# Second output banks, an earlier norm and transfers moved ahead in the first feed-forward group of a sandwich block

## What is computed

```python
x = x + layernorm(attn(layernorm(x), Wq, Wk, Wv, Wo))
x = x + layernorm(ffn(layernorm(x), gate_cp, up_cp, down_cp))
```

## Time and profile before

| | before |
|---|---|
| median of 3 runs | 719.9 us (717.62 to 720.74) |
| the profiled execution | 722.85 us |
| its span | 721.0 us |
| TensorE busy | 667.9 us, 93% of the span |
| VectorE busy | 491.9 us, 68% |
| GpSimd busy | 440.1 us, 61% |
| ScalarE busy | 373.6 us, 52% |
| DMA, mean | 159 GB/s |
| granted TensorE clock, mean | 0.972 of full |

### The profile page before, as it was taken

The page is one execution under the profiler, slowest core; times in us unless marked ns, Lnnn a source line. Parts: engine busy times, 40 slices in busy tenths (PEclk is TensorE's granted clock), DMA queues, the critical chain, the costliest instruction groups (busy, mean ns, idle before and its releaser), DMA issues. The chain is left out here.

```text
span 721.0 us, 16306 instructions
## 1 busy us (share of the span) xinstructions
PE 667.9 (93%) x5872; PEld 468.7 (65%) x5872; DVE 491.9 (68%) x977; ACT 373.6 (52%) x651; POOL 440.1 (61%) x615
## 2 busy tenths in 40 slices
PE   5898899999999999999977689999999999999896
PEld 3686686878778786877863346565665656665464
DVE  7657964479635885366577677877878788865542
ACT  3532332333323332333347567778777787777642
POOL 6098958628585576970245456667666666666542
PEclk9898999999999999999998799999999999999999
DMA  6835447415482246830299564657475757646222
GB/s 216 327 99 177 152 162 257 151 30 174 167 263 85 90 146 190 282 103 16 66 248 282 124 171 119 175 163 191 149 193 160 190 147 188 155 132 183 79 78 98
DMA packets 65549, 114.98 MB, mean 159 GB/s; under 512 B 12624, under 2 KB 29136, under 8 KB 65488
## 3 DMA queue, kind: packets, MB, share of 16 engines
q1 hardware_dynamic: 65488, 114.16, 53.8%
HBM read 81.76 MB, written 32.37 MB: 158 GB/s over the span
## 5 line engine op out<-in xcount | busy, mean ns | idle before, releaser
L1420 POOL TENSOR_TENSOR act<-inter,act 128x512 f16<-128x512 f32 x128 | 157.9, 1240 | 93.4 <-ACT act L1460 93.3
L1464 ACT ACTIVATE gated<-gbank,c_gate 128x512 f32<-128x512 f32 x128 | 87.4, 683 | 56.9 <-PE gbank L1622 56.9
L1537 DVE SCALAR_TENSOR_TENSOR inter<-ubank,c_up,gated 128x512 f32<-128x512 f32 x128 | 95.8, 748 | 28.4 <-ACT gated L1464 24.2
L1664 PE MATMUL ybank<-down,act 128*128 128x160 f16 x512 | 109.8, 234 | 0.0
L1666 PE MATMUL ybank<-down,act 128*128 128x160 f16 x512 | 109.1, 233 | 0.0
L1665 PE MATMUL ybank<-down,act 128*128 128x160 f16 x512 | 109.1, 233 | 0.0
L1460 ACT CAST act<-inter 128x512 f16<-128x512 f32 x128 | 78.0, 609 | 4.2 <-DVE inter L1537 4.2
L1664 PEld LDWEIGHTS ybank<-down,act 128*128 128x128 f16 x512 | 50.0, 98 | 29.5 <-issue 25.7
L1622 PE MATMUL ubank<-z,s_all 128*32 128x512 f16 x512 | 52.4, 399 | 17.9 <-DVE inter L1537 16.6
L1622 PE MATMUL gbank<-z,s_all 128*32 128x512 f16 x512 | 52.9, 403 | 5.6 <-DMA z<-token_features 3.8
L687 DVE SCALAR_TENSOR_TENSOR tu_lo<-chain,tu_hi 128x512 fp32r<-128x512 f32 x32 | 22.1, 691 | 45.0 <-ACT tu_hi L555 44.9
(11 more groups left out here) (196 smaller groups left out, 1911.4 us busy)
## 6 DMA issues: line engine op xcount, KB each, us to landing
x_ln<-x SPq DMA_DIRECT2D x64, 256.0 KB, 3.5
z<-token_features SPq DMA_DIRECT2D x64, 256.0 KB, 5.1
job<-job_in SPq DMA_DIRECT2D x24, 640.0 KB, 4.1
shared<-x SPq DMA_DIRECT2D x32, 256.0 KB, 2.8
x<-shared SPq DMA_DIRECT2D x32, 256.0 KB, 2.0
token_features<-z_hi SPq DMA_DIRECT2D x32, 256.0 KB, 3.8
x_res<-x SPq DMA_DIRECT2D x32, 256.0 KB, 2.9
out<-x_res SPq DMA_DIRECT2D x32, 256.0 KB, 3.0
```

Source lines behind the costliest of these rows:

```text
L1420: pool.tensor_tensor(hidden[par][:, i, TOK:2 * TOK], inter[:, i % INTERS, :], hidden[par][:, i, 0:TOK], ALU.subtract).then_inc(inter_ready, 1)
L1464: act.activation(gated[:, slot % 2, :], gbank[:], ACT.Silu, scale=c_gate[:]).then_inc(silu_done, 1)
L1537: dve.scalar_tensor_tensor(out=inter[:, i % INTERS, :], in0=ubank[:], scalar=c_up[:], in1=gated[:, i % 2, :], op0=ALU.mult, op1=ALU.mult). ...
L1664: pe.matmul(out, hidden[par][:, r, high], box[:, 0], start=False, stop=False)
```

## The change

Five edits, all in the lists' order or in the banks:

- In group 0 the odd steps 3 to 15 put gate and up in ybank0 and ybank1 (`pair_of`). From step 4 to 15 gate waits for the silu of step n-2 and up for the product of step n-2. Step 3 waits in their place for attention's last read of those banks (`y_read`). The silu of steps 3 to 15 waits also for the product of n-2, since its own output has two buffers. Steps 16 and 17 wait in full again.
- In group 0 the norm of tile m+1 moves from the end of step s == 3 to s == 2, behind the copy of the turned tile m, and its high and low halves move from s == 0 of the next round to s == 3, ahead of tile m's `z_high` and `z_low`.
- `load_z` of group 0's first half moves from t == 4 to t == 2 of attention's stores.
- x_ln of tile 8 goes ahead of the twelve reads of the down weights (now `jobs`); and in round 2 of every group `load_z` of the second half goes behind that round's output store and reload.
- ScalarE waits for `wov_done` 1 instead of 2 ahead of the exponentials.

```diff
--- before.py
+++ after.py
@@ -351,7 +351,7 @@
                         feats.load(sp, x1_t, XR + t, t)
                     if not more and t == 0:
                         feats.spill(sp, 1, 0)
-                    if not more and t == 4:
+                    if not more and t == 2:
                         sp.wait_ge(chain_done, b * CHAIN + 3 * K)
                         ffn_in.load_z(sp, feats, 0, 0, 0)
                 if more:
@@ -594,7 +594,7 @@
                         turned_hi(b, m)
                     if isinstance(b, int) and b == 0 and m == 2:
                         wov_hi(1)
-                act.wait_ge(wov_done, 2)
+                act.wait_ge(wov_done, 1)
                 if not more:
                     feats.high(act, 0)
                 for m in range(K):
@@ -1311,6 +1311,10 @@
         o_normed = sem("o_normed")
         out_ready = sem("out_ready")
 
+        def pair_of(n):
+            return ybank if isinstance(n, int) and n in range(3, I, 2) else (gbank, ubank)
         def schedule(engine, quad, loop=True):
 
 
@@ -1356,25 +1360,32 @@
                 else:
                     load_res(g + 1, q - 2)
 
-            def regroup(g, par, half, loads_before):
-                spread(g, par, half, loads_before)
-                ffn_in.load_z(sp, feats, g, par, half)
             def spread(g, par, half, loads_before):
 
                 sp.wait_ge(z_loaded[1 - par][half], loads_before * 64)
                 feats.spill(sp, half, g, 1 - par)
+            def jobs():
+                attention.jobs_stored(sp)
+                for b in range(I // PER):
+                    sp.dma_start(w_box[:, b * PER:(b + 1) * PER], d_dram[b][:, 0:PER]).then_inc(ffn_in.down_loaded, 16)
+                    for c in range(2):
+                        bank, quarter = (2 * b + c) // 4, (2 * b + c) % 4
+                        sp.dma_start(w_mom[:, bank, :, quarter * P:(quarter + 1) * P], d_dram[b][:, PER + c, :, 0:P]
+                                     ).then_inc(ffn_in.down_loaded, 16)
+                attention.all_stored(sp)
 
             def quad(g, par, count, j, made, begun, more):
                 for ahead in ((0,), (1, 2, 3), (), ())[j] if more else ():
                     m = g * Q + ahead + AHEAD + 2
                     sp.wait_ge(feats.h_normed, m - RING + 1)
                     feats.load(sp, x1_t, m, (ahead + AHEAD + 2) % RING)
+                if isinstance(g, int) and g == 0 and j == 0:
+                    jobs()
                 last = isinstance(g, int) and g == GROUPS - 1
                 if j == 2 and not last:
-                    regroup(g + 1, 1 - par, 1, count)
+                    spread(g + 1, 1 - par, 1, count)
                 for i in range(4 * j, 4 * j + 4):
                     for before, q in outputs(g, i, 2):
                         finish(before, q)
@@ -1384,7 +1395,8 @@
                 if j == 1 and not last:
                     if isinstance(g, int) and g == 0:
                         spread(g + 1, 1 - par, 0, count)
-                    ffn_in.load_z(sp, feats, g + 1, 1 - par, 0)
+                if j in (1, 2) and not last:
+                    ffn_in.load_z(sp, feats, g + 1, 1 - par, j - 1)
 
             sp.wait_ge(feats.h_normed, Q)
             feats.load(sp, x1_t, Q + 3, 3)
@@ -1394,14 +1406,6 @@
             attention.store(sp)
             for q in range(2):
                 load_res(0, q)
-            attention.jobs_stored(sp)
-            for b in range(I // PER):
-                sp.dma_start(w_box[:, b * PER:(b + 1) * PER], d_dram[b][:, 0:PER]).then_inc(ffn_in.down_loaded, 16)
-                for c in range(2):
-                    bank, quarter = (2 * b + c) // 4, (2 * b + c) % 4
-                    sp.dma_start(w_mom[:, bank, :, quarter * P:(quarter + 1) * P], d_dram[b][:, PER + c, :, 0:P]
-                                 ).then_inc(ffn_in.down_loaded, 16)
-            attention.all_stored(sp)
             schedule(sp, quad)
             finish(GROUPS - 2, Q - 1)
             reload(GROUPS - 2, Q - 1)
@@ -1461,7 +1465,9 @@
 
             def silu_at(n, slot):
                 act.wait_ge(gate_done, n + 1)
-                act.activation(gated[:, slot % 2, :], gbank[:], ACT.Silu, scale=c_gate[:]).then_inc(silu_done, 1)
+                if isinstance(n, int) and 3 <= n < I:
+                    act.wait_ge(inter_done, n - 1)
+                act.activation(gated[:, slot % 2, :], pair_of(n)[0][:], ACT.Silu, scale=c_gate[:]).then_inc(silu_done, 1)
 
             def moment_hi(g, bank):
 
@@ -1504,8 +1510,11 @@
                         moment_hi(g - 1, 1)
                     if i == I - 1:
                         moment_hi(g, 0)
-                    if s == 0 and made:
+                    first = isinstance(g, int) and g == 0
+                    if s == 0 and made and not (first and j):
                         feats.high(act, g * Q + j + AHEAD)
+                    if s == 3 and first and j < Q - 1:
+                        feats.high(act, j + AHEAD + 1)
                     if isinstance(n, int) and n == 2 * Q + 3:
                         attention.jobs_stored(act)
                     if s == 3 and made:
@@ -1534,7 +1543,7 @@
                 dve.wait_ge(up_done, n + 1)
                 if not (isinstance(n, int) and n < INTERS):
                     dve.wait_ge(inter_ready, n - INTERS + 1)
-                dve.scalar_tensor_tensor(out=inter[:, i % INTERS, :], in0=ubank[:], scalar=c_up[:],
+                dve.scalar_tensor_tensor(out=inter[:, i % INTERS, :], in0=pair_of(n)[1][:], scalar=c_up[:],
                                          in1=gated[:, i % 2, :], op0=ALU.mult, op1=ALU.mult).then_inc(inter_done, 1)
 
             def moment_lo(g, bank):
@@ -1579,13 +1588,18 @@
                         o_stats(before, q)
                     for before, q in outputs(g, i, 2):
                         o_finish(before, q)
-                    if s == 0 and made:
+                    first = isinstance(g, int) and g == 0
+                    if s == 0 and made and not (first and j):
                         feats.low(dve, m)
+                    if s == 2 and first:
+                        feats.norm(dve, m + 1, (j + 1 + AHEAD) % RING)
+                    if s == 3 and first and j < Q - 1:
+                        feats.low(dve, m + 1)
                     if s == 0 and begun:
                         feats.stats(dve, m + 1, (j + AHEAD + 1) % RING, loads)
                     if s == 3 and made:
                         feats.z_low(dve, m, (j + 2) % Q, z_banks, par if j < 2 else 1 - par)
-                    if s == 3 and begun:
+                    if s == 3 and begun and not first:
                         feats.norm(dve, m + 1, (j + 1 + AHEAD) % RING)
 
             product(0, 0)
@@ -1614,8 +1628,13 @@
                 if i % HALF == 0:
                     pe.wait_ge(z_loaded[par][i // HALF], count * 64)
                 side, c = i // HALF, i % HALF
-                for w, bank, free, done in ((GATE, gbank, silu_done, gate_done), (UP, ubank, inter_done, up_done)):
-                    if not (isinstance(n, int) and n == 0):
+                gate, up = pair_of(n)
+                if isinstance(n, int) and n == 3:
+                    attention.y_read(pe)
+                for w, bank, free, done in ((GATE, gate, silu_done, gate_done), (UP, up, inter_done, up_done)):
+                    if isinstance(n, int) and 3 < n < I:
+                        pe.wait_ge(free, n - 1)
+                    elif not (isinstance(n, int) and n in (0, 3)):
                         pe.wait_ge(free, n)
                     for u in range(4):
                         rows = slice(32 * u, 32 * u + 32)
```

## The result

| | before | after |
|---|---|---|
| median | 720.32 us (717.62 to 724.32, 4 runs) | 713.43 us (712.47 to 713.94, 4 runs) |
| ratio | 1 | 0.9897, 95% interval 0.9873 to 0.9922 |
| profiled execution, its span | 722.85, 721.0 us | 713.47, 711.6 us |
| VectorE's last instruction starts at | 717.78 | 708.37 |

The change makes the kernel 6.9 us faster by the medians. Between the two profiled executions it is 9.4 us, because that of before lies 2.5 us above its median. Three marks on VectorE's timeline split the 9.41 us by which the last instruction moved. The first statistics of y in attention's last body moved from 354.13 to 350.24, 3.89 us. From there to the first moments of group 0 (`mom_lo`, the low part of its first moment products, which VectorE forms near the group's end) it takes 64.00 instead of 67.61 us, 3.61 less.

The account below looks back on a forecast made before the run. Later groups were taken as bound by TensorE's own work, leaving gains in group 0, its change-over and attention's first body. 1.2 + 6.5 = 7.7 us took the median from 719.9 to 712.2 us, range 709.5 to 716.8.

Parts of the forecast that it names:

- Body 0: Attention's first body: the first exponential starts up to 3.2 us earlier, GpSimd's list limits the gain to 1.2 us.
- rival 3: Attention's first body gives nothing, eaten by GpSimd's list and a clock drop: 713.4 us, or 1.6 more; chance 0.17.
- Change-over: From attention to group 0: z read 3.9 us earlier, TensorE's wait for it gone, silu and product 1.1 us earlier.
- the prediction's lower bound for this term: Change-over from attention to group 0: gain of nothing, if the residual reads that z's reads pass come late.
- Round 0: Group 0's first round: the product of step 6 comes 2.2 us earlier, 1.1 more than the start gave.
- Round 1 and 2: Group 0's rounds: norm and halves lie beside copy and feature products, so a round takes 6.35 us instead of 8.73.
- x_ln of tile 8: Group 0, round 1: with its read ahead of the down weights, VectorE's stall of 2.98 us is gone or nearly.
- Crowding: Group 1's input: x_ln reads of tiles 9 to 11 still under way add 0.7 us to its load.
- A new wait for z: Group 1's first gate, round 3: TensorE's wait of 0.60 us becomes some 5 us and caps the gain.
- Later groups: Groups after group 0: nothing is shorter, and the second half's load moving by about a microsecond costs nothing.
- The page against the banks: A skill page reporting no further gain from PSUM double-buffering; by its rule group 0's rounds stay at 8.73 us.
- the first rival: Banks and new order do nothing for group 0's rounds, another wait takes the loop's place: 714.0 us; chance 0.15.

Follow-up runs that it names:

- e8_z_t3: Changed kernel with group 0's load of z one step later on SyncE's list, behind the first residual read and ahead of the second: 713.37 us, 0.9894 of before.
- e2_z_t4: Changed kernel with group 0's load of z back behind the two residual reads, at step 4 instead of 2: 714.34 us, 0.9919 of before.
- e5_x8_behind: Changed kernel with the read of x_ln for tile 8 again behind the twelve reads of the down weights: 718.58 us, 0.9961 of before.
- e10_no_round_edits: Changed kernel with both round edits undone (single banks, old place of norm and halves): 715.30 us, 0.9931 of before.
- e6_regroup: Changed kernel with the second half's load of group input again directly behind its spread, ahead of that quarter's output stores: 716.80 us, 0.9945 of before.
- e3_one_bank: Changed kernel with single banks for gate and up in group 0 again, new order of norm and halves kept: 714.10 us, 0.9915 of before.
- e7_wov_only: Kernel before with only the wait ahead of the first exponential changed, to one part of Wv instead of both: 719.63 us, 0.9986 of before.

## Why the prediction was right

The time, 713.43 against 712.2, came out because terms that were too large and terms that were too small made up for each other. Step by step:

- *Body 0, 1.2 us.* Right in size by the first statistics of y (1.5 on average) and by the medians (1.0 and 1.7). What it lacked is the clock: I had it as a loss in rival 3, "or 1.6 more". In the profiles with the edit it mostly stayed at 2.4 GHz through the products of y, and A gained 1.4 more, by luck as far as is shown; the profile of after has the earliest A of all. That GpSimd's list was the bound fits the 1.5 of a possible 3.2, and no run tests it.
- *Change-over, 1.1 us.* Wrong. The step that failed is "The other reads and stores behind z are 1.9 us later in SyncE's list; VectorE uses the first of them more than 5 us after". The issue did come 1.94 us later against the first statistics of y (15.25 instead of 13.31). What I left out is the landing: behind the four reads of z, this read took 6.8 us instead of 3.5, so it landed 5.2 us later in all, and VectorE waited 2.35 us for it. In e8_z_t3, where it goes ahead of z, it took 4.1 us and nobody waited. e2_z_t4 shows the sum as nothing; the prediction's lower bound for this term had named the reason.
- *Round 0, another 1.1 us.* Wrong in sign. Product 6 moved by 3.06 us where the last body's first statistics had moved by 3.89, so change-over and round 0 together lost 0.8. "VectorE is packed up to product 3" took the lengths from a trace in which GpSimd came second. And product 4 came 1.67 us behind product 3 instead of the 0.9 that I gave it, 0.95 of it a wait for its silu.
- *Round 1 and 2, 6.35 us.* Measured 7.27. The terms that were mis-sized are the norm and the low half, which I hid beside other work at their old lengths. The norm takes 1.37 instead of 0.55 beside GpSimd. 7.27 - 0.82 is 6.45, so the rest of the sum was nearly right. I had looked for a wait on another engine and not at the length of VectorE's own list.
- *x_ln of tile 8.* Right: no stall, and e5_x8_behind shows it worth 3.5 us, more than the 2.98 that I took from the old stall; its own stall was 3.3 us.
- *Crowding, 0.7 us.* Nothing, from z_lo of tile 7 to the gate: 12.85 against 12.84.
- *A new wait for z of some 5 us.* Right, 4.12. It does cap what the rounds can give on TensorE, as e10_no_round_edits shows.
- *Later groups, nothing.* Wrong. "Nothing there is shorter" overlooked that the moved load had a stall behind it in the last groups, 1.9 us (e6_regroup). I read waits for z there, and not the residual's.

By the profiles, 3.89 + 3.61 + 1.91 = 9.41 us stand against 1.2 + 6.5 + 0 = 7.7.

**The page against the banks.** The changed kernel's rounds did shorten, so the first rival as I priced it fell. The 0.91 us that I read there as silu's wait is VectorE's wait for silu. But most of the gain is the order's: on top of it, the banks are worth 0.07 us a round in the net (e3_one_bank). The Trainium skill (TensorE: Matmul & The Clock Gate, "HAM oscillation — how this bites in real kernels") reports that double-buffering in PSUM gave no further gain to a kernel whose loop had already been reordered against its DMA waits. By that net number the trace agrees. Without the new order it doesn't: banks alone took the mean round from 8.67 to 8.05.

## What to carry to other kernels

Read a queue that works in order for what stands *behind* a transfer, at both ends of the move, and count when it lands, not only when it is issued: here one residual read that was passed by four others stalled VectorE for 2.35 us, and one that was freed gave 1.9 us in a place that nobody had aimed at. A list that is packed to the last instruction has to be summed with the lengths that its instructions have in their new company, not with the old ones. And a second pair of banks took a wait of 0.66 us out of the round here without shortening it, because another instruction grew by as much; try the reordering alone first, and look at where the wait went.

## What was not expected of the hardware

Two engines lengthen each other's instructions, and a start earlier by 0.01 us decides which one waits. When GpSimd's low part is first, VectorE's residual addition takes 1.56 to 1.68 instead of 0.74 us. When VectorE is first by 0.1 us or less, GpSimd's takes 1.65 to 1.69 instead of 1.16, as in e8_z_t3 (by 0.46 us, in e2_z_t4 and e7_wov_only, it takes 1.30):

```profile
379.15 1.65 POOL L1424 TENSOR_TENSOR act<-inter,act 128x512 f16<-128x512 f32 x1 [1.69 <-ACT act L1464]
```

VectorE's L231 had started there 0.10 us earlier. VectorE's products, whose in0 lies in PSUM, keep 0.73 to 0.75 us beside GpSimd. The Trainium skill (SBUF — State Buffer, "Who interferes with whom") has this as a port pair that the first to start holds for its whole instruction, while the other blocks. These rows agree: L231 ends 0.54 or 0.55 us after GpSimd's end in all five profiles, whenever it started. I did not apply it to the instructions that the change moved beside GpSimd.

TensorE's clock makes the first body differ from one execution to the next by as much as some of the edits: the same kernel idled for 1.76 and 1.77 us ahead of y, kept 2.4 GHz in one execution and was for a part at 1.2 in the other, and A differed by 2.05 us, 1.5 of it from the first statistics of y on.
